# Another beginning for a fused attention and FFN layer: input in smaller units, key weights split by themselves

## The reference

```
n   = LN(x)
q, k, v = n @ Wqkv.T + b            # 16 query heads, 8 key heads of 128; 4 value heads of 256
p1, p2  = causal softmax of q.k / sqrt(128), for the two members of each head pair
o   = (p1 - lam * p2) @ v           # lam from four small vectors
o   = o / rms(o) * subln_w * (1 - LAMBDA_INIT)
x1  = x + LN(o @ out_w.T + out_b)
h   = silu(gate) * up               # gate, up: two projections to 1024 of a Hadamard-transformed LN(x1)
out = x1 + LN(Hadamard(h) @ W_down.T * scales)
```

## Time and profile before

| | |
|---|---|
| median of 3 runs | 1367.39 us (1366.65 to 1367.54) |
| the profiled execution's own time | 1367.04 us |
| its span | 1365.2 us |
| busy: TensorE, weight loads | 1349.7, 1203.5 us |
| busy: VectorE, ScalarE, GpSimd | 1035.3, 888.2, 798.5 us |
| matmuls (transposes among them) | 8342 |

### The profile page before, as it was taken

How to read it: one execution, slowest core, us unless ns; L and a number is a source line. 1 busy time by engine, 2 the same in 40 slices (tenths; PEclk the granted TensorE clock), 3 DMA queues, 4 the chain that set the end, 5 groups by cost and what they waited for, 6 DMA issues and landing times.

```text
span 1365.2 us, 26616 instructions
## 1 busy us (share of the span) xinstructions
PE 1349.7 (99%) x8342; PEld 1203.5 (88%) x8342; DVE 1035.3 (76%) x2717; ACT 888.2 (65%) x2494; POOL 798.5 (58%) x1223
## 2 busy tenths in 40 slices
PE   9999999999999999999999999999999999999998
PEld 8889999889989999889899999889889898888787
DVE  8878778877787778866877778867788888866545
ACT  5766666765676766665676666665667777765441
...
DMA packets 9753, 18.51 MB, mean 14 GB/s; under 512 B 912, under 2 KB 7312, under 8 KB 9104
## 3 DMA queue, kind: packets, MB, share of 16 engines
...
## 4 chain that ended last, share of the span: by engine, by line
PE 84%; DVE 8%; ACT 3%; issue 2%; POOL 2%; DMA 0%; ACTq 0%; POOLq 0%; DVEq 0%
PE turn_bank L719 9%; PE score_bank L697 8%; PE score_bank L699 8%; PE score_bank L698 8%; PE score_bank L814 7%; PE turn_bank L721 4%; PE sum_bank L719 4%; PE turn_bank L706 4%; PE proj_bank L719 3%; PE proj_bank L765 3%; PE turn_bank L779 2%; PE sum_bank L721 2%; PE turn_bank L765 2%; PE sum_bank L706 2%; PE proj_bank L706 2%
## 5 line engine op out<-in xcount | busy, mean ns | idle before, releaser
L849 ACT ACTIVATE e<-score_bank,negmx 128x512 f32<-128x512 f32 (+2 forms) x640 | 395.2, 626 | 89.0 <-DVE negmx L1076 87.4
L1322 POOL TENSOR_TENSOR e<-e,e 128x512 f32<-128x512 f32 (+3 forms) x256 | 293.2, 1145 | 21.3
L1072 DVE TENSOR_REDUCE mx<-score_bank 128x1 f32<-128x512 f32 (+1 forms) x384 | 241.3, 636 | 39.1 <-PE score_bank L699 37.6
L697 PE MATMUL score_bank<-k_hi,q_hi 128*128 128x512 f32 (+2 forms) x640 | 258.8, 404 | 2.7 <-DVE q_lo L1104 1.0
L1310 POOL TENSOR_SCALAR ratio<-s,inv_s,neg_lam 128x1 f32<-128x1 f32 x128 | 43.4, 339 | 364.8 <-DVE inv_s L1054 364.5
L699 PE MATMUL score_bank<-k_hi,q_lo 128*128 128x512 f32 (+2 forms) x640 | 231.3, 361 | 0.0
L719 PE MATMUL turn_bank<-v_hl,pT_hi 128*128 128x512 f32 x633 | 230.2, 397 | 0.9 <-DVE pT_lo L1082 0.6
L698 PE MATMUL score_bank<-k_lo,q_hi 128*128 128x512 f32 (+2 forms) x640 | 230.7, 361 | 0.0
L1319 POOL TENSOR_SCALAR e<-e,ratio 128x512 f32<-128x512 f32 (+3 forms) x256 | 183.8, 718 | 12.0
L721 PE MATMUL turn_bank<-v_hl,pT_lo 128*128 128x256 f32 x633 | 177.5, 280 | 0.0
L1067 DVE CUSTOM_DVE_ANT_0 score_bank<-score_bank,mask 128x384 f32<-128x384 f32 (+3 forms) x256 | 142.8, 558 | 41.7 <-PE score_bank L699 39.8
...
## 6 DMA issues: line engine op xcount, KB each, us to landing
...
out_dram<-e SPq DMA_DIRECT2D x16, 128.0 KB, 1.7
...
```

Source lines behind the costliest of these rows:

```text
L697: pe.matmul(bank[:, 0:w], qh, kh, start=True, stop=False)
L849: act.activation(e, S[k % NS][:, 0:w], ACT.Exp, bias=negmx[:, d % 2, m, s:s + 1], accum_out=ssum[:, d % 4, s, m, c:c + 1]).then_inc(s_act, 1)
L1072: dve.tensor_reduce(mx[:, d % 2, m, s, c:c + 1], S[k % NS][:, 0:w], X, ALU.max)\
L1322: pool.tensor_tensor(a, a, b, ALU.add).then_inc(p_pool, 1)
```

## The change

The input is loaded, normalised and turned in units of their own: 2, 2, 4, 4 and 4 tiles (`NORM_UNITS`). An X step turns both channel halves of two tiles, where it turned one half of four, still with four transposes. The first four X steps use the score banks. Three of the 16 tiles (1, 5, 10) are normalised by VectorE, after the power and ahead of the shift, the rest by ScalarE. The key weights are loaded in two pieces on two queues and split alone; the value weights come later and are split in a step WV, the low part by GpSimd. The query weights move from ScalarE's DMA queue to SP's. The last four tiles and the small early tensors lie under the last value tiles. There are 22 + 6 fillers for 38 + 8 + 8. The order of the beginning is new; the steps X 6, X 7 and WO of the first group stand in halves 3 and 5 (letter A), and its keys and values spread to half 10. In the first group the pair of tiles 6 to 9 comes second. Some letters change places in the patterns of later halves and in the lists of the FFN. Waits for keys and values are issued when a later one is needed for the first time, no longer for every step of a group's first duo.

```diff
+NORM_UNITS = ((0, 2), (2, 2), (4, 4), (8, 4), (12, 4))
+FIRST_ORDER = (3, 4, 7, 2, 5, 1, 6, 0)
-HALVES = ('TSTTTSSSPoTSQTOPPP', 'STSTSOTTTSPSoQPPP')
+HALVES = ('TSTTSTSSPoTSQTOPPP', 'STSTSOSTTTPSoQPPP')
 HEAD = {
-    3: 'TQSKSTPSSSP', 4: 'TSSVTSSTTPSoQPPTOTP', 5: 'TVSTSPOTSQSSoTPVPPT'}
+    3: 'TQSTSSPSASP', 4: 'TSTSTSSPToTPSQTPOP', 5: 'TSTAASSAOTSQPSoTPKTPP', 6: 'STSTSSTQTSPPoPTPTKO',
+    7: 'STSoSOSTPSTQPPTPT', 8: 'TSTSSTSToPTPQSPTVOP', 9: 'STSSTSOoTPSTQVTPVPP', 10: 'TSTSSSTPSToQTTPPPO'}
 TURN_OF_GROUP = {
-    0: 'TSSKTPKoTSSPSTQTPKTOPK', 2: 'TTSSTSVVSQVSVoTPPVTTPVPOV', 3: 'TSSVTSOTTPSoTSQPPP',
-    27: 'STSTTkSSPOTSoQwPTPP', 28: 'STTTSSTSPoSQTOPTPP', 31: 'KSTTTSKSPKSTOToSKPPQP'}
+    0: 'TSSKTPKoTSSPSTQTPKTOPK', 2: 'TTSSTSVVSQVSVoTPPPVTTVOPV', 3: 'TSSTSOVTTPSoTSQPPP',
+    27: 'STTSTkSSPOTSoQwPTPP', 28: 'STTTSSTSPoSQTOTPPP', 31: 'KSTTSKTPKSSTOToSKPPQP'}
...
 FIRST_STEPS = (
-    ("LN", 0), ("LN", 1), ("NX", 0), ("WK", 0), ("NX", 1), ("IDLE", 38), ("X", 0), ("X", 1), ("IDLE", 8),
-    ("X", 2), ("X", 3), ("IDLE", 8), ("WQ", 0), ("LN", 2), ("K", (0, 1, 0)), ("K", (0, 0, 0)),
-    ("QP", (0, 1, 0)), ("K", (0, 0, 1)), ("NX", 2), ("QP", (0, 1, 1)), ("S", (0, 0, 0)), ("X", 4), ("X", 5),
-    ("S", (0, 0, 1)), ("K", (0, 1, 1)), ("LN", 3), ("WO", (0, 1)), ("QP", (0, 0, 0)), ("K", (0, 1, 2)),
-    ("K", (0, 0, 2)), ("S", (0, 0, 2)), ("NX", 3), ("WO", (0, 0)), ("S", (0, 0, 3)), ("QP", (0, 0, 1)),
-    ("V", (0, 0)), ("X", 6), ("S", (0, 0, 4)), ("X", 7), ("V", (0, 1)), ("S", (0, 1, 0)), ("S", (0, 1, 1)),
...
+    ("LN", 0), ("IDLE", 22), ("LN", 1), ("NX", 0), ("LN", 2), ("NX", 1), ("WK", 0), ("X", 0), ("X", 1),
+    ("IDLE", 6), ("NX", 2), ("K", (0, 0, 0)), ("LN", 3), ("X", 2), ("K", (0, 1, 0)), ("X", 3), ("WQ", 0),
+    ("K", (0, 0, 1)), ("NX", 3), ("K", (0, 1, 1)), ("X", 4), ("X", 5), ("QP", (0, 1, 0)), ("QP", (0, 1, 1)),
+    ("S", (0, 0, 0)), ("S", (0, 0, 1)), ("LN", 4), ("QP", (0, 0, 0)), ("K", (0, 0, 2)), ("WV", 0),
+    ("K", (0, 1, 2)), ("S", (0, 0, 2)), ("S", (0, 0, 3)), ("NX", 4), ("S", (0, 0, 4)), ("QP", (0, 0, 1)),
+    ("S", (0, 1, 0)), ("V", (0, 0)), ("S", (0, 1, 1)), ("V", (0, 1)), ("S", (0, 1, 2)), ("S", (0, 1, 3)),
+    ("V", (0, 2)), ("LAM", None), ("V", (0, 3)), ("S", (0, 1, 4)), ("QP", (1, 1, 0)), ("S", (1, 0, 0)),
...
+NX_BY_VECTOR = (1, 5, 10)
...
+    late = [("WO", (0, 1)), ("WO", (0, 0)), ("X", 6), ("X", 7)]
...
-                sp.dma_start(x_in[:, 0:2, :], x_tiles[:, 0:2, :]).then_inc(x_landed[0], 16)
-                sp.dma_start(x_in[:, 4:6, :], x_tiles[:, 4:6, :]).then_inc(x_landed[1], 16)
-                sp.dma_start(w_raw[:, :, BANK:2 * BANK], w_qkv[0][:, :, BANK:2 * BANK]).then_inc(first_w_landed, 16)
-                sp.dma_start(x_in[:, 8:12, :], x_tiles[:, 8:12, :]).then_inc(x_landed[2], 16)
+                sp.dma_start(x_first[:, 0:1, :], x_tiles[:, 0:1, :]).then_inc(x_landed[0], 16)
+                sp.dma_start(x_first[:, 2:3, :], x_tiles[:, 2:3, :]).then_inc(x_landed[1], 16)
+                sp.dma_start(w_raw[:, 0, BANK:BANK + HID], w_qkv[0][:, 0, BANK:BANK + HID]).then_inc(wk_landed, 16)
+                sp.dma_start(x_first[:, 4:6, :], x_tiles[:, 4:6, :]).then_inc(x_landed[2], 16)
                 sp.dma_start(col[:, :], cols[:, :]).then_inc(cols_landed, 16)
+                sp.dma_start(w_raw[:, :, 0:BANK], w_qkv[0][:, :, 0:BANK]).then_inc(wq_landed, 16)
+                sp.dma_start(x_first[:, 8:12, :], x_tiles[:, 8:12, :]).then_inc(x_landed[3], 16)
+                sp.dma_start(w_raw[:, :, BANK + HID:], w_qkv[0][:, :, BANK + HID:]).then_inc(wv_landed, 16)
+                sp.dma_start(x_late[:, :, :], x_tiles[:, 12:16, :]).then_inc(x_landed[4], 16)
...
-                act.dma_start(x_in[:, 2:4, :], x_tiles[:, 2:4, :]).then_inc(x_landed[0], 16)
-                act.dma_start(x_in[:, 6:8, :], x_tiles[:, 6:8, :]).then_inc(x_landed[1], 16)
-                act.dma_start(w_raw[:, :, 0:BANK], w_qkv[0][:, :, 0:BANK]).then_inc(w_landed, 16)
-                act.dma_start(x_in[:, 12:16, :], x_tiles[:, 12:16, :]).then_inc(x_landed[3], 16)
+                act.dma_start(x_first[:, 1:2, :], x_tiles[:, 1:2, :]).then_inc(x_landed[0], 16)
+                act.dma_start(x_first[:, 3:4, :], x_tiles[:, 3:4, :]).then_inc(x_landed[1], 16)
+                act.dma_start(w_raw[:, 1, BANK:BANK + HID], w_qkv[0][:, 1, BANK:BANK + HID]).then_inc(wk_landed, 16)
+                act.dma_start(x_first[:, 6:8, :], x_tiles[:, 6:8, :]).then_inc(x_landed[2], 16)
...
                     elif kind == "WK":
                         if what == 0:
-                            act.wait_ge(first_w_landed, 16)
+                            act.wait_ge(wk_landed, 32)
+                            act.activation(wkv_hi[:, :, 0:HID], w_raw[:, :, BANK:BANK + HID], ACT.Copy).then_inc(w_hi, 1)
...
+                    elif kind == "WV":
+                        act.wait_ge(wv_landed, 16)
+                        act.activation(wkv_hi[:, :, HID:], w_raw[:, :, BANK + HID:], ACT.Copy).then_inc(wv_hi, 1)
...
                     elif kind == "LN":
-                        t = slice(4 * what, 4 * what + 4)
-                        pool.wait_ge(stats_ready, 4 * what + 4)
+                        first, n = NORM_UNITS[what]
+                        t = slice(first, first + n)
+                        pool.wait_ge(stats_ready, first + n)
                         pool.tensor_scalar(var_eps[:, t], mv[:, t, 1], 1.0, EPS, ALU.mult, ALU.add)\
                             .then_inc(rstd_step, 1)
+                        pool.wait_ge(rstd_step, 3 * what + 1)
+                        pool.tensor_tensor(rstd[:, t], var_eps[:, t], half_neg[:, 0:n], ALU.pow).then_inc(rstd_step, 1)
                         pool.tensor_scalar(neg_mean[:, t], mv[:, t, 0], -1.0, 0.0, ALU.mult, ALU.add)\
                             .then_inc(rstd_step, 1)
-                        pool.wait_ge(rstd_step, 3 * what + 2)
-                        pool.tensor_tensor(rstd[:, t], var_eps[:, t], half_neg[:, :], ALU.pow).then_inc(rstd_step, 1)
```

More of the change, by code:

```diff
@@ L265, in attention_steps @@
                 queue = {"T": turns, "S": scores, "P": products, "Q": extra, "K": keys, "V": values,
-                         "w": split_q, "k": split_k, "N": norms, "f": folds, "H": hadamard, "b": added_up}[what]
+                         "w": split_q, "k": split_k, "N": norms, "f": folds, "H": hadamard, "b": added_up,
+                         "A": late}[what]
                 if queue:
                     emit(*queue.pop(0))
-        for what in (*turns, *scores, *products, *keys, *extra):
+        for what in (*turns, *scores, *products, *extra):
             emit(*what)
-        del keys[:]
-        if at == 5:
-            assert not values
+        if group > 0:
+            for what in keys:
+                emit(*what)
+            del keys[:]
+        if at == (10 if group == 0 else 5):
+            assert not (keys or values or late)
     assert not (values_due or exps_due or factors_due or mixes_due or norms or folds or added_up)
@@ L529, in build @@
                         last_first_visit = what
+            by_pool = []
+            for what in n_v:
+                by_pool.append((by_pool or [0])[-1] + (what not in BY_VECTOR))
             WORK = (T[0], T[1], R, O)
@@ L538, in build @@
                     use = ("PV", duo_chunks(what[0])[what[1]][0])
-                if kind not in ("T", "PV", "OT", "OP", "QP", "K", "V", "Z", "F", "X", "DN"):
+                if kind not in ("T", "PV", "OT", "OP", "QP", "K", "V", "Z", "F", "X", "DN") or kind == "X" and what < NS:
                     continue
```

153 lines of the change are left out of this document (92 added, 61 removed), and 33 rows, old and new, of tables (FIRST_STEPS, SCALAR_LAGS, VECTOR_LAGS, WITH_GATED).

## The result

| | us (median, lowest to highest) | runs | span of the profiled execution |
|---|---|---|---|
| before, on the same chip | 1367.30 (1366.65 to 1367.62) | 9 | 1365.2 |
| after | 1371.22 (1369.54 to 1372.44) | 9 | 1369.4 |

A forecast was written before the change was run, and what follows sets the result against it. TensorE, busy for 1349.7 of 1365.2 us, was taken to bound the kernel, with VectorE's queue pacing 20 to 40 us. The terms -0.7 + 1.7 - 2.2 - 0.3 = -1.5 us on 1367.04 gave 1365.5, range 1362.3 to 1369.0.

The forecast's parts named there:

- term D: Rest of the kernel, after 60 us: small waits at group ends and in the FFN lists shift; -0.3 us, bounds -2 and +2.
- A, first key projection: Kernel start: first key projection at 11.8 us instead of 13.36, useful work 0.7 us ahead; -0.7 us, bounds 0 and -1.9.
- rival at 0.12: Kernel start: TensorE, pausing in its warm-up, is still at the lower clock level at 11.8 us; +1.1 us, 1368.1; chance 0.12.
- B, to the first score: First key projection to first score: TensorE waits for the chain after X3 and the last query projection; +1.7 us.
- C, first scores to half 5: First scores to 60 us: VectorE's full queue is relieved, value projections cover waits; -2.2 us of 2.7 lost there.
- the third unit's tile (0.4 us): Before the first key projection: VectorE has this work ahead of xT_lo, booked at 0.4 us.
- Half the pattern edit is empty: Patterns of later halves: letters without a chunk to turn emit nothing, the swapped turns and scores cost 0 us.
- 1362.4: Rival for the whole kernel: all the waits of the first scores and group turns go; -4.7 us; chance 0.25.
- 1370.4: Rival for later halves: moved values and 32 swapped halves wait 0.1 to 0.2 us each; +3.3 us; chance 0.06.

The follow-up runs named there:

- e1: The changed kernel with more fillers: 5 between X 0 and X 1, and 24 instead of 6 after X 1; 1369.02 us, ratio 1.0017.
- e10: e7 with the turn of tiles 6 and 7 (X3) ahead of K(0,1,0) instead of behind it; 1365.82 us, ratio 0.9992.
- e13: e10 with the evictions of X2 and X3 ahead of the split of K(0,0,0) on ScalarE and VectorE; 1365.7 us, ratio 0.9989.
- e6: The kernel before with the change's later patterns and FFN lists, but the old half 127 and the old beginning; 1364.87 us, ratio 0.9985.
- e12: The kernel before with all later patterns of the change, new half 127 among them, and the old beginning; 1367.99 us, ratio 1.0007.
- e5: The kernel before with only the change's new pattern of half 127; 1367.81 us, ratio 1.0006.
- e2: The changed kernel with the old pattern of half 127 put back; 1367.35 us, ratio 1.0008.
- e7: The changed kernel with the fillers of e1 and the old pattern of half 127; 1365.82 us, ratio 0.9991.
- e3: The changed kernel with one lag taken out: VectorE's part of X 1 ahead of its part of NX 2; 1370.23 us, ratio 1.0021.

## Why the prediction was wrong

Two steps failed above all. The sum put the lower clock level at nothing, and it cost 2.6 us; and term D put all of the rest at -0.3 us, while the new pattern of half 127 alone cost 3.1 us. Its terms against the traces, in us of lost time against the kernel before:

| term | forecast | measured | from |
|---|---|---|---|
| A, first key projection | -0.7 | -0.1 | 13.36 - 12.38 = 0.98 earlier, less 0.87 of turning not yet done |
| clock | 0, rival at 0.12 | +2.6 | e1: 13.74 - 11.10 |
| B, to the first score | +1.7 | +2.0 | first score +4.55, less A and clock |
| C, first scores to half 5 | -2.2 | -0.85 | +4.55 to +3.70 |
| D, half 5 to half 127 | -0.3, all of it | -2.3 | +3.70 to +1.43 |
| D, behind half 127 | in it | +2.7 | +1.43 to +4.12 |
| sum | -1.5 | +4.1 | spans: 1369.4 - 1365.2 = 4.2 |

- *The clock.* The forecast had no term for it. The rival with the lower level named the kind of loss and its cause, pauses of TensorE, and got a chance of 0.12. Its way there was another: it asked whether TensorE would reach the full level by 11.8 us. TensorE reached it by 8.90 and lost it again at 11.3, in the pause of 2.2 us that the late third unit made. The size agrees (forecast +2.6 net, from 6.2 us at the level; measured 2.6, from 5.7 us), but the 6.2 us were those of the first warm-up, so that is in part luck. A reading beside it was off: the counts of the earlier trace rows are of all matmuls that touch a stretch, and 4 and 9 start there, not 6 and 11; the spacing, on which the argument rests, is right. The Trainium skill, "TensorE: Matmul & The Clock Gate", "What's actually happening", has the low level as the default that activity releases; the trace agrees with it: 0.213 us between transposes up to 7.6 us, 0.109 us from 8.90, and a granted clock of 0.50 behind the pause, from 12.4 us.
- *Term A, the step of the landing.* The first two units were there in time (the turn of the second began at 8.90 us, forecast 9.5 to 10.1): GpSimd took 1.50 us for a unit of two tiles, not 1.95, because the power took 0.72 us and not 1.04, so its time does shrink somewhat with the tiles. What failed is that the third unit's place in VectorE's queue was not followed: it was booked as "the third unit's tile (0.4 us)", while its four statistics wait for a load that lands at 7.64 us (7.4 to 8.9 in the other profiles), with the split, both xT_lo and the first projection 4.74 us behind. That pushed 11.8 to 12.38 and made the pause, with only six fillers in it.
- *Term B* was right as a sum, and its reason was half right: 1.50 us are lost ahead of K(0,0,1) as forecast, but in e10 and e13 what holds K(0,0,1) is the order of the queues, VectorE's wait for k_hi with xT_lo behind it, and not the length of the chain from X3.
- *Term C.* The waits up to half 2 do go (from +4.55 to +1.45, 3.1 us), more than forecast; then the new order puts a wait of 1.39 us ahead of S(1,0,4), and half 5 stands at +3.70. The reading "less work in VectorE's queue, so no waits" named no instruction that would wait next.
- *Term D* failed twice. "Half the pattern edit is empty" is true for HALVES, but e6 has 2.2 us from the patterns, more than half of it in the last group, where the small waits had been left unread. And the new pattern of half 127 was read as letters: that it moves two exponentials behind the first silu, so that ScalarE switches its function table twice more, was to be seen in the order of its queue. The runs price it: 3.1 us (e12 against e6, medians), of which 2.2 show in profiles without the lower level, and 0.9 us where the exponentials stand directly behind the silu (e5).
- *Sums.* Two of the rivals' times, 1362.4 and 1370.4, lie 0.1 us above their own sums (1367.04 - 4.7 and 1367.04 + 3.3); nothing hangs on it.

By medians against the kernel before: later patterns -2.2 us (e6), half 127 +3.1 (e12 less e6), beginning +3.0 (after, +3.9, less e12, +0.9). Of the beginning, the repair of the clock brings 1.9 us (e2 at +0.7, e7 at -1.2); a profile shows 2.6, so not every execution loses all of it. The mean granted clock of the single executions fits: 0.995 to 0.997 in all nine after, 0.999 or 1.000 in all eleven of e7 and of e6, and in e3 and e12 the longer executions are, but for one, those with the lower clock. The spreads fit too (2.9 us after, 1.5 in e7, 1.1 in e6; 2.5 in e1 and 2.6 in e12, which keep the late pause). Where in an execution without a trace the level fell is not shown.
